# One transformer block on one core: key and value rotations computed elementwise instead of by matmul

## The reference, cut to what matters

```python
h = _layernorm(x) * (1 + ca) + sa              # per batch: vectors sa, ca of 256 channels
q, k, v = (givens_rotate(rot_w[m], h) for m in range(3))
# givens_rotate: for each channel pair (0,1), (2,3), ...
#   y0 = c * x0 - s * x1 ;  y1 = c * x1 + s * x0     with (c, s) from rot_w, normalised
attn = softmax((2 + 2 * q @ k.T) / scale + bias)
ave = attn @ v
x = x + ga * ave / sqrt(|ave . ave|)
h = _layernorm(x) * (1 + cb) + sb
x = x + gb * (experts(h) + shared_expert(h))   # experts: top-64 tokens of each batch and expert
```

## Time and profile before

| what | value |
|---|---|
| median of three runs | 2466.16 us (2465.39 to 2470.37) |
| span of the profiled execution | 2465.3 us |
| part A / part B, about | to 1310 us / from there |
| TensorE, TensorE weight load busy | 96%, 85% of the span |
| VectorE, ScalarE, GpSimd busy | 64%, 42%, 47% of the span |

### The profile page before, as it was taken

The page is one execution under the profiler, slowest core; times in us unless marked ns, Lnnn a source line. Parts: engine busy times, 40 slices in busy tenths (PEclk is TensorE's granted clock), DMA queues, the critical chain, the costliest instruction groups (busy, mean ns, idle before and its releaser), DMA issues.

```text
span 2465.3 us, 40995 instructions
## 1 busy us (share of the span) xinstructions
PE 2372.3 (96%) x14388; PEld 2086.3 (85%) x14388; DVE 1567.9 (64%) x3198; ACT 1032.8 (42%) x1912; POOL 1150.4 (47%) x997
## 2 busy tenths in 40 slices
PE   6999999999998999999987999999999999999997
PEld 5888888888887888888876888888888888888886
DVE  6677767778776877788846455555554545555553
ACT  3545545444553545545442333333333333333332
POOL 1233333333332333333352666666666666666664
PEclk9999999999998999999998999999999999999999
DMA  2111111111111111111115444443444444434433
GB/s 90 53 44 59 51 60 60 52 51 57 54 61 44 60 43 60 52 60 60 59 62 90 86 90 82 88 84 66 79 84 87 86 85 88 84 60 86 84 62 43
DMA packets 78506, 167.03 MB, mean 68 GB/s; under 512 B 11744, under 2 KB 46720, under 8 KB 78368
## 3 DMA queue, kind: packets, MB, share of 16 engines
q0 software_dynamic: 49152, 67.14, 16.7%
q1 hardware_dynamic: 29216, 97.85, 11.8%
HBM read 97.71 MB, written 67.24 MB: 67 GB/s over the span
## 4 chain that ended last, share of the span: by engine, by line
PE 84%; DVE 6%; issue 4%; POOL 2%; DMA 1%; ACT 1%; SPq 0%; DVEq 0%; POOLq 0%; ACTq 0%
PE ps L349 26%; PE ps L351 26%; PE ps L350 26%; PE ps L501 2%; DVE stage L856 2%; PE ps L387 1%; DVE bn_stats L758 1%; PE ps L420 1%; DMA stage<-in_wd 1%; DVE x_t L753 1%; PE ps L442 1%; DVE hidden L753 1%; POOL rstd L1144 1%; POOL out L1209 1%; ACT x_t L693 0%
## 5 line engine op out<-in xcount | busy, mean ns | idle before, releaser
L349 PE MATMUL ps<-x_t,weights 128*128 128x512 f32 x1536 | 617.3, 402 | 23.2 <-DVE hidden_f L1111 13.3
L350 PE MATMUL ps<-x_t,weights 128*128 128x512 f32 x1536 | 602.5, 392 | 0.0
L351 PE MATMUL ps<-x_t,weights 128*128 128x512 f32 x1536 | 601.8, 392 | 0.0
L1209 POOL DMA_INDIRECT out<-x_rows,step_token x256 | 418.1, 1633 | 333.9 <-DVE x_rows L1090 275.4
L349 PE MATMUL ps<-weights,hidden 128*128 128x256 f32 x1536 | 435.8, 284 | 8.7 <-POOL hidden L1148 5.6
L351 PE MATMUL ps<-weights,hidden 128*128 128x256 f32 x1536 | 436.1, 284 | 0.0
L350 PE MATMUL ps<-weights,hidden 128*128 128x256 f32 x1536 | 436.0, 284 | 0.0
L1111 DVE TENSOR_TENSOR hidden_f<-gelu,ps 128x512 f32<-128x512 f32 x256 | 175.7, 686 | 379.0 <-ACT gelu L733 348.1
L733 ACT ACTIVATE gelu<-ps 128x512 f32<-128x512 f32 x256 | 152.8, 597 | 535.8 <-PE ps L351 508.4
L349 PEld LDWEIGHTS ps<-x_t,weights 128*128 128x128 f32 x1536 | 290.6, 189 | 83.6 <-DVE hidden_f L1111 13.5
L1148 POOL TENSOR_TENSOR hidden<-hidden_f,hidden 128x512 fp32r<-128x512 f32 x128 | 165.5, 1293 | 408.7 <-ACT hidden L647 408.7
(11 more groups left out here) (174 smaller groups left out, 4436.9 us busy)
## 6 DMA issues: line engine op xcount, KB each, us to landing
x_rows<-in_x SPq DMA_DIRECT2D x32, 512.0 KB, 3.5
pairs<-mod_rows SPq DMA_DIRECT2D x32, 512.0 KB, 4.3
h_rows<-stage SPq DMA_DIRECT2D x32, 512.0 KB, 2.6
out<-y_rows SPq DMA_DIRECT2D x32, 512.0 KB, 2.9
stage<-in_wg SPq DMA_DIRECT2D x16, 512.0 KB, 3.4
stage<-in_wd SPq DMA_DIRECT2D x16, 512.0 KB, 4.4
stage<-in_wu SPq DMA_DIRECT2D x16, 512.0 KB
x_rows<-h_rows,step_token POOLq DMA_INDIRECT x256
```

Of the source, the lines that this page charges most:

```text
L349: pe.matmul(o, lhs(HI), rhs(HI), start=start, stop=False)
L350: pe.matmul(o, lhs(HI), rhs(LO), start=False, stop=False)
L351: return pe.matmul(o, lhs(LO), rhs(HI), start=False, stop=stop)
L1209: pool.indirect_dma_start(out=out_rows, out_offset=bass.IndirectOffsetOnAxis(ap=ICUR[g][:, t:t + 1], axis=0), in_=X1[:, g % 2, t * D:(t + ...
```

## The change

Nothing of the rotations is left on TensorE. What the changed kernel does:

- Transposed rows (`x_transposes`) are taken by parity: `XN` is written as [tile, parity, pair], so that after the transposes the two channels of a pair stand on the same partition, in the two halves `k` of the tile. The matrix products sum over channels, and so don't mind the order; `attention_out` puts the channels back by a strided write, and the modulation vector GA is stored by parity.
- Keys: ScalarE makes a scaled and shifted copy of the transposed rows (`KTF`, two more activations), VectorE adds the other half times a sine per partition (`k_rotate`, two instructions of 128x512 with one operand in PSUM), ScalarE copies the high part (`k_split`), VectorE takes the rest (`k_split_lo`).
- Values stay as rows: GpSimd multiplies the normalised rows by a coefficient row (`v_scaled`), multiplies the swapped halves by another (`v_swapped`, two instructions of 128x512), adds a third row (`v_shifted`) and the swapped product (`v_summed`). ScalarE copies the high part (`v_split`) and GpSimd takes the rest (`v_rest`). The six coefficient rows of a batch (384 KB over 128 partitions) are worked out once at the start, stored in DRAM, and loaded for each batch by the queue of SyncE (`v_rows`), behind the load of the modulation vectors.
- `ln1_apply` moves from VectorE to GpSimd, with a stride-2 read. The high part of h1 moves from VectorE to ScalarE.
- On TensorE `x_transposes(i+1)` now stands ahead of the first half of attention times values, and waits for the splits of two of the four attention tiles only; the wait for the values' splits moves from `scores` to `a_times_v`.
- The prologue's matmul with the swap matrix and the chain of small instructions that built the rotation matrices go; per-partition coefficients take their place. K_T and V now lie in the space of the second weight buffer, which is free in part A.

```diff
         def _(sp):
...
+            def v_rows(n, q):
+                sp.dma_start(VMOD[:, q, :, :].rearrange("p m i -> p (m i)"),
+                             v_dram[bass.ds(n, 1), :].to_broadcast((P, NV))).then_inc(vmod_in[q], 16)
...
                     wait(sp, y_ready, i - 1)
                     sp.dma_start(out_v[i - 2], Y[:, :, :].rearrange("p t d -> p (t d)")).then_inc(y_stored, 16)
...
                     sp.dma_start(MODB[:, p, :, :].rearrange("p m d -> p (m d)"),
                                  mod_dram[bass.ds(i, 1), :].to_broadcast((P, NMOD * D))).then_inc(mod_in[p], 16)
+                if valid(i + 1) and not at(i, -1):
+                    wait(sp, v_ready, i)
+                    v_rows(i + 1, 1 - p)
...
             def x_transposes(n):
                 wait(pe, xn_ready, n + 1)
-                wait(pe, at_hi, n * T)
-                wait(pe, at_lo, n * T)
+                wait(pe, at_hi, n * T - 2)
+                wait(pe, at_lo, n * T - 2)
...
             def iteration(i, p, half, rounds=(), finish=None, start=None):   # TensorE
-                if valid(i):
-                    k_and_v(i)
                 if valid(i - 2):
                     gate_up(i - 2, 3)
...
                     gate_transposes(i - 1)
-                if valid(i):
-                    a_times_v(i, 0)
                 if valid(i + 1):
                     x_transposes(i + 1)
...
+                if valid(i):
+                    a_times_v(i, 0)
...
             def h1_modulate(n):                                              # ScalarE
...
+                for k in range(KD):
+                    last = act.activation(KTF[:, k, :], PC[:, k * S:(k + 1) * S], ACT.Identity,
+                                          bias=KC[:, B0 + k, bass.ds(n, 1)], scale=KC[:, A0 + k, bass.ds(n, 1)])
+                last.then_inc(kt_ready, 1)
+                wait(act, h1f_ready, n + 1)
+                act.copy(H1_T[:, HI, :, :], H1_F).then_inc(h1_hi, 1)
...
+            def k_rotate(n):                                                 # VectorE
+                dve.wait_ge(kt_ready, n + 1)
+                for k in range(KD):
+                    last = dve.scalar_tensor_tensor(KTF[:, k, :], PC[:, (1 - k) * S:(2 - k) * S],
+                                                    KC[:, S0 + k, bass.ds(n, 1)], KTF[:, k, :], ALU.mult, ALU.add)
+                last.then_inc(k_rot, 1)
+            def k_split_lo(n):
+                dve.wait_ge(k_hi, n + 1)
+                split_lo(K_T[:, LO, :, :], KTF[:, :, :], K_T[:, HI, :, :]).then_inc(k_lo, 1)
...
+            def ln1_apply(n, p):                                             # GpSimd
+                wait_apart(pool, xt_done, n)
+                wait_apart(pool, rs1, n + 1)
+                for t in range(T):
+                    last = pool.tensor_scalar(XN[:, t, :, :], X[:, p, t * D:(t + 1) * D].rearrange(
+                        "p (i j) -> p j i", j=2), MV[0][:, t, 0:1], RS[0][:, t:t + 1], ALU.subtract, ALU.mult)
+                last.then_inc(xn_ready, 1)
+            def v_scaled(n, q, loads):
+                wait(pool, vmod_in[q], loads * 16)
+                wait(pool, xn_ready, n + 1)
+                wait(pool, v_hi, n)
+                wait(pool, v_lo, n)
+                pool.tensor_tensor(VF[:, :, :, :].rearrange("p t j i -> p t (j i)"),
+                                   XN.rearrange("p t j i -> p t (j i)"),
+                                   by_tile(flat(VMOD[:, q, A0:A1 + 1, :])), ALU.mult).then_inc(v_step, 1)
...
                 if valid(i - 1):
                     rstd(1, mv2, ve2, rs2, i - 1)
+                if valid(i):
+                    v_rest(i)
...
                 if valid(i + 1):
                     rstd(0, mv1, ve1, rs1, i + 1)
+                    ln1_apply(i + 1, 1 - p)
                 if valid(i - 2):
                     pool.wait_ge(y_read, i - 1)
                     pool.tensor_tensor(Y[:, :, :].rearrange("p t d -> p (t d)"),
...
+                if valid(i + 1):
+                    v_scaled(i + 1, 1 - p, half + 1 + p)
                 if valid(i - 1):
                     hidden_lo(i - 1, 0)
+                if valid(i + 1):
+                    v_swapped(i + 1, 1 - p)
+                    v_shifted(i + 1, 1 - p)
+                if valid(i - 1):
                     hidden_lo(i - 1, 1)
+                if valid(i + 1):
+                    v_summed(i + 1)
```

More of the change, by code:

```diff
@@ L44 @@
 C_EVEN, C_ODD, C_SIGN, C_BASE = range(2 * P, 2 * P + 4)
+PAIR = D // 2
+A0, A1, S0, S1, B0, B1 = range(6)
+NV = 6 * PAIR
 C_HALF = C_BASE + NG
@@ L426, in a_times_v @@
                     pe.wait_ge(mods_raw, 1)
+                if half == 0:
+                    wait(pe, v_hi, n + 1)
+                    wait(pe, v_lo, n + 1)
                 for t in (2 * half, 2 * half + 1):
@@ L640, in h1_modulate, with k_split, v_split @@
                 last.then_inc(h1f_ready, 1)
+                if at(n, 0):
+                    act.wait_ge(kc_ready, 1)
+                wait(act, k_hi, n)
+                wait(act, k_lo, n)
+                for k in range(KD):
[4 more added lines that the diff above has]
+                act.copy(H1_T[:, HI, :, :], H1_F).then_inc(h1_hi, 1)
+            def k_split(n):
+                wait(act, k_rot, n + 1)
+                act.copy(K_T[:, HI, :, :], KTF[:, :, :]).then_inc(k_hi, 1)
+            def v_split(n):
+                wait(act, v_ready, n + 1)
+                act.copy(V[:, HI, :, :].rearrange("p t d -> p (t d)"),
+                         VF[:, :, :, :].rearrange("p t j i -> p (t j i)")).then_inc(v_hi, 1)
             def hidden(n, fc):
@@ L702, in iteration @@
                     hidden(i - 1, 0)
+                if valid(i + 1):
+                    h1_modulate(i + 1)
+                if at(i, -1):
+                    act.wait_ge(vc_ps, 1)
+                    act.copy(v_mods, PG[0:B, 0:NV]).then_inc(v_mods_ready, 1)
                 if valid(i):
@@ L712, in iteration @@
                     hidden(i - 1, 2)
+                if valid(i + 1) and not at(i, -1):
+                    v_split(i + 1)
                 if at(i, B):
@@ L784, in _ @@
             ln1_stats(0, 0, 1)
+            dve.wait_ge(rot_rn, 1)
+            for m in range(2):
+                link(dve.tensor_tensor(CS[:, m, :], ROT[:, :, m], RN[:, :], ALU.mult))
+            dve.wait_ge(scal_in, 32)
+            r2, cz, ncz = SCB[:, 3:4], SCB[:, 4:5], SCB[:, 5:6]
+            link(dve.reciprocal(SCB[:, 2:3], SCB[:, 0:1]))
+            link(dve.tensor_scalar(r2, SCB[:, 2:3], 2.0, None, ALU.mult))
+            link(dve.tensor_tensor(cz, r2, SCB[:, 1:2], ALU.add))
+            link(dve.tensor_scalar(ncz, cz, -1.0, None, ALU.mult))
@@ L789, in _ @@
+            dve.tensor_scalar(flat(SACA[:, 1, :, :]), PG[:, 2 * B:4 * B], 1.0, None,
                               ALU.add).then_inc(saca_ready, 1)
[L791 to L819 removed]
@@ L1041, in iteration @@
                     weights_lo(i, (2, 3))
-                if valid(i + 1):
-                    ln1_apply(i + 1, 1 - p)
-                if at(i, -1):
-                    rotations()
                 if at(i, 0):
@@ L1064, in iteration @@
                     hidden(i - 1, 1)
+                if valid(i + 1):
+                    k_split_lo(i + 1)
                 if len(rounds) > 1:
@@ new lines, in v_swapped, with v_shifted @@
+            def v_swapped(n, q):
+                for j in range(2):
+                    last = pool.tensor_tensor(VS[:, :, j, :], XN[:, :, 1 - j, :], by_tile(VMOD[:, q, S0 + j, :]),
+                                              ALU.mult)
+                last.then_inc(v_step, 1)
+            def v_shifted(n, q):
+                wait(pool, v_step, n * 3 + 2)
+                pool.tensor_tensor(VF[:, :, :, :].rearrange("p t j i -> p t (j i)"),
+                                   VF[:, :, :, :].rearrange("p t j i -> p t (j i)"),
+                                   by_tile(flat(VMOD[:, q, B0:B1 + 1, :])), ALU.add).then_inc(v_step, 1)
@@ new lines, in v_summed, with v_rest @@
+            def v_summed(n):
+                wait(pool, v_step, n * 3 + 3)
+                pool.tensor_tensor(VF[:, :, :, :].rearrange("p t j i -> p (t j i)"),
+                                   VF[:, :, :, :].rearrange("p t j i -> p (t j i)"),
+                                   VS[:, :, :, :].rearrange("p t j i -> p (t j i)"), ALU.add).then_inc(v_ready, 1)
+            def v_rest(n):
+                wait(pool, v_hi, n + 1)
+                pool.tensor_tensor(V[:, LO, :, :].rearrange("p t d -> p (t d)"),
+                                   VF[:, :, :, :].rearrange("p t j i -> p (t j i)"),
+                                   V[:, HI, :, :].rearrange("p t d -> p (t d)").bitcast(F32),
+                                   ALU.subtract).then_inc(v_lo, 1)
```

203 lines of the change are left out of this document (94 added, 109 removed).

## The result

The changed kernel takes 2829.81 us (median of 4 runs, 2822.57 to 2830.77), the kernel before 2466.06 (4 runs, 2465.39 to 2470.37): a ratio of 1.1459, with a 95% interval of 1.1445 to 1.1474. It is slower by 14.6%. The forecast was 2757 us with a range of 2590 to 2830: the direction and the mechanism came out, the size was 73 us short. The measured time lies 0.2 us inside the upper end of that range, which is luck, and outside the narrower 2700 to 2805 that the prediction called this case's own.

A forecast was written before the change was run, and what follows sets the result against it. A ring through GpSimd's in-order list was to set the pace: steps of 44.9 us plus meetings of 2.3 and 1.2 give 48.4 a batch against 38.7; 2465.3 + 291 + 0.9 = 2757 us, range 2590 to 2830.

The forecast's parts named there:

- this case's own: The range for the ring with the meetings: 46.5 (short load) to 50 us a batch, 2700 to 2805; chance 0.57.
- the ring: GpSimd's in-order list with its waits, once around from `h2_ready(i-1)` to `h2_ready(i)`: 44.9 us a batch, 48.4 with meetings.
- `ln1_apply` on GpSimd: Four `tensor_scalar` of 128x256 on GpSimd, not in the trace: 2.2 us, the middle between 1.39 on VectorE and 2.95.
- wait for coefficient rows: GpSimd stands still ahead of `v_scaled` for a load third in SyncE's queue: 6.3 us, from below 4.0.
- The meetings: VectorE and GpSimd exclude each other: `v_rest` with `ln2_centre` 2.3 us, `k_split_lo` with `v_scaled` 1.2, each from below 0.
- Rival 1: Same ring without the meetings: 44.9 us a batch, 2652 us; 2559 with load at 4.0 and `ln1_apply` at 1.4; chance 0.26.
- (a): TensorE: without the rotations between them, `gate_up(i-2, 3)` waits for GELU and product of `gate_up(i-1, 2)`: 1.5 us.
- GpSimd's work: GpSimd's busy time a batch after the change: 13.4 + 2.2 + 5 x 2.40 + 2.6, about 30 us.
- rival 2: TensorE keeps the pace: 37.8 us a batch, 2439 us, faster; decides once the ring is under 37.8; chance 0.07.
- The prologue: Chain for coefficient rows ends near 40 us, the first `a_times_v` came at 45: 0 taken, 10 us at most.
- Rival 3: TensorE's clock falls as it idles: at 0.66 all along, with both stalls, 54.4 us a batch, 2937 us; chance 0.06.
- (b): TensorE: `x_transposes` loses the cover of `a_times_v` and waits for `ln1_apply`: 2.0 us.

The follow-up runs named there:

- e1: Changed kernel with the next batch's coefficient rows loaded at the start of SyncE's iteration, ahead of the load of x: 2687.65 us, 1.0900.
- e2: Changed kernel with `v_rest` ahead of the second norm's root on GpSimd instead of behind it: 2757.32 us, 1.1176.
- e6: As e5, with `v_summed` and `v_split` behind the next iteration's sum of x1, and `v_rest` back behind the second norm's root: 2490.09 us, 1.0091.
- e5: Changed kernel with the edits of e1 and e2, `ln1_apply` back on VectorE, and GpSimd's output sum behind `v_scaled`: 2568.93 us, 1.041.
- e4: Kernel before, with one matmul in place of three in the rotations, leaving out the products with the rests: 2424.32 us, 0.983.
- e9: As e6, with GpSimd's output sum moved from behind `v_scaled` to ahead of the first norm's root: 2460.98 us, 0.9969.

## Why the prediction was right, and where its size was off

Term by term, from the timelines above (one period, 612.2 to 662.3):

| step of the ring | forecast | measured |
|---|---|---|
| h2 ready to first norm's root (626.95 to 634.52) | 7.4 | 7.6 |
| `ln1_apply` on GpSimd | 2.2 | 5.1 |
| output rows' sum | 2.4 | 2.4 |
| wait for coefficient rows | 6.3 | 6.2 |
| `v_scaled` to output factor, meeting included | 15.0 | 14.2 |
| `attention_out` and sum of x1 | 4.4 | 4.2 |
| `ln2_stats` to `ln2_apply`, meeting included | 10.7 | 10.5 |
| sum | 48.4 | 50.2 |

- **What bounds it.** Right. The ring through GpSimd's order sets the pace with no engine full, and e1, e2 and e6 show it from three sides: each takes a step off the ring that no matmul has a part in, and the time falls by 142, 72.5 and 79 us (the last from e5).
- **The step that was mis-sized: `ln1_apply` on GpSimd.** The prediction took "the middle, 2.2" between 1.4 and 2.95. It takes 4.90 for the four (and 0.2 ahead of them): outside both ends, since both came from other instructions, VectorE's own and GpSimd's `tensor_tensor`, and the form itself had no row. That is 2.9 us a batch; the other terms took 1.1 of it back, and the mean period is 0.2 under the one shown. The miss of 73 us adds up: 30 x (49.9 - 48.4) = 46 here, 12 in the prologue, 6 in the tail, 8 between profiled execution and median. TensorE's wait ahead of `x_transposes` is 3.85 for the same reason, not 2.0. An upper end from a different form of instruction was no upper end.
- The Trainium skill (GPSIMD Engine Reference, "3.1 Elementwise") has 1.03 cycles an element for a body of up to two operations, and about 2.6 for a `tensor_tensor`, which reads two inputs. From the first the prediction worked out an estimate of 1.6 us for the four. The measurement decides against it here: 4.90, and 0.94 each even with one operation.
- **The meetings.** Right in size. 2.3 was forecast for `ln2_centre` beside `v_rest`: 3.90 - 1.67 = 2.23 in the trace, and 2.4 a batch when e2 took it away. At the keys' rests 1.2 was forecast, and it is 1.0, as `hidden_lo` at 2.29 in place of 1.29, not as a late next pass. The Trainium skill (SBUF — State Buffer, "Who interferes with whom") says that the later of the two waits out the other; the trace agrees in both directions. Rival 1, the ring without meetings, falls with e2.
- **The coefficient rows.** Wait and place right (6.17; third in the queue; 5.06 from issue to landing). What the prediction did not have is that the wait also kept GpSimd and VectorE apart: taking it away was worth 5.4 in the usual iteration and 4.7 on average, not 6.2.
- **TensorE's own stalls.** 1.41 for (a), forecast 1.5. That the removal gives at most 4.0 a batch was right as a bound; e4 shows that of 2.41 freed 1.1 arrive in the usual iteration.
- **GpSimd's work.** The prediction added "5 x 2.40" for new passes over 1024 elements; there are four (`v_scaled`, `v_shifted`, `v_summed`, `v_rest`), so its sum is 28 and not 30, and "five a batch, four on the ring" in rival 2 is miscounted too. The ring's own sum has each pass once, and the forecast doesn't depend on it.
- **The prologue**, costed at nothing with at most 10: it is 11.7. GpSimd's second `ln1_apply` stands at 46.21 with 7.61 us, beside VectorE's rests of the weights (L795 on SBUF operands), 5.4 over the 2.2 forecast. The other 6 us were not taken apart.
- **The tail**, said to be as before, is some 6 us longer (355.3 - 337 - 11.7). Of these, 4.3 lie inside part B, which the change doesn't touch: from the first to the last of its output DMAs it takes 1123.1 us (1687.5 to 2810.6), before 1118.8 (1336.7 to 2455.5). No run looked into the cause.
- **The median** lies 9.2 us over the profiled span of 2820.6, where the forecast added 0.9: the profiled execution was the quickest of the four (2822.57).
- **Rival 3, TensorE's clock.** It did fall: granted 0.90 from 600 to 700, a mix of 2.4 and 1.2 GHz, at 77% busy with gaps of 0.5 to 4 us, where it was 1.00 before. It did not set the pace. From 300 to 600 us TensorE is busy for 231 of 300 us at 0.88, so 38.5 of the 49.9 us of a batch, where the forecast had about 34; an estimate of its own period is then 38.5 with the two stalls, 1.4 for (a) and 4.9 for (b) with the longer `ln1_apply` (2.0 + 2.9): 45 us, still under the ring. e1 takes 5.4 us from the usual iteration without touching its work, and the clock came back by itself to 0.99 in e9, at 91% busy. Rival 2 needed a ring under 37.8, and it was 50.

## What to carry to other kernels

Work that leaves a full engine joins the in-order list of another. Before moving it, follow the batch once around all lists, every instruction and every DMA issued behind a semaphore of that list included, and compare the sum with the full engine's period; that sum was right here to 4% (with 2.9 us too little in one term and 1.1 too much in the others), and no busy share shows it. Price each instruction on its new engine in its own form, since a bound from a neighbouring form can fail on both ends. And look at where GpSimd waits already: the output sum moved into such a gap, one statement of the kernel before, gained 0.9%, more than the best version with the whole change.

## What the hardware showed that was not expected

- GpSimd's `tensor_scalar` (f32, two per-partition operands) takes 1.24 us for 128x256, 1.22 with packed input, 0.94 with one operation; four on VectorE take 1.38 to 1.39.
- GpSimd is held up by VectorE as much as the other way: passes of 1.29 took 2.29, of 2.40 up to 3.36, where one of VectorE's rests with two SBUF operands, having waited for the pass before, was served first.
- The size of VectorE's instruction does not matter for its wait. L919, on 4 elements a partition, took 1.25 us (mean before 0.154) and ended at 652.77, with `hidden_lo` ending at 652.75. A COPY of 16 elements (L1016, one operand) took 1.67 in place of 0.165 and ended at 641.98, with the output sum ending at 641.95. So in this trace not only instructions with two operands stand still, as `ln1_apply` had shown on VectorE. That GpSimd held them up is read from the ends, which fall together.
- Not every pass of GpSimd holds VectorE up. Beside its `ln1_apply` (634.73 to 639.63) VectorE's product of two SBUF operands at 637.66 (L988, 64 elements) takes 0.22, its usual time (median 0.225); so it does beside the `ln1_apply` of most other batches, and 0.45 to 0.48 in a few. One batch earlier the COPY of L1016 stands inside `ln1_apply` (at 588.49, from 584.19 to 589.09) and takes 0.16. VectorE's waits shown in this document are beside GpSimd's instructions with two inputs; why these differ, no run shows.
